# The end of a head pair's attention on VectorE in 18 pieces instead of 10, and a long projection group put first in a pair's second cycle

## The reference

```python
x = x + attn_a(layernorm(x))      # causal attention, 16 heads of 64
x = x + ffn(layernorm(x))         # named f1 in the kernel
x = x + attn_b(layernorm(x))      # a retention scan along the tokens, gated; no scores
x = x + ffn(layernorm(x))         # named f2 in the kernel

# attn_a: q, k, v = x Wq', x Wk', x Wv', split into 16 heads
scores = where(causal, q k' / 8, -inf)
out = (softmax(scores) v) Wo'

# ffn: also attention, not causal, over its 2048 tokens. Each of its four projections
# has a main weight plus two experts of rank 16 chosen from the mean of the tokens:
q = (x Wqm' + gate-weighted (x Vg') Sg Ug' + b) / 8      # k, v likewise
out = o_projection(softmax(q k') v)
```

## Time and profile before

| What | Value |
|---|---|
| profiled execution, span of core 5 | 2594.22 us, 2592.5 us |
| spans of the 8 cores | 2567.9 to 2592.5 us |
| mean granted TensorE clock of the cores | 0.944 to 0.951 |
| PE busy | 2201.5 us, 85% |
| ACT busy | 1498.3 us, 58% |
| DVE busy | 1317.0 us, 51% |
| POOL busy | 635.0 us, 24% |
| DMA | 58 GB/s in the mean |

### The profile page before, as it was taken

The page is one execution under the profiler, slowest core; times in us unless marked ns, Lnnn a source line. Parts: engine busy times, 40 slices in busy tenths (PEclk is TensorE's granted clock), DMA queues, the critical chain, the costliest instruction groups (busy, mean ns, idle before and its releaser), DMA issues.

```text
span 2592.5 us, 39690 instructions; the slowest of 8 cores (2567.9 to 2592.5 us)
## 1 busy us (share of the span) xinstructions
PE 2201.5 (85%) x13480; PEld 766.5 (30%) x13480; DVE 1317.0 (51%) x2018; ACT 1498.3 (58%) x1494; POOL 635.0 (24%) x762
## 2 busy tenths in 40 slices
PE   4888799998699989879899599996989989788886
PEld 2322222223342222222222244443422222222222
DVE  4367635656453444434554567775445454433443
ACT  1234377773007777879999032221057777899991
POOL 4244333434111111112212323333021211021112
PEclk9989899999699999999999899997999999999998
DMA  8111322224400000012211531135200000021003
GB/s 173 25 25 25 62 46 65 66 74 129 148 9 24 25 26 25 17 49 58 58 42 50 130 73 66 65 114 154 74 25 26 25 25 17 17 74 33 33 33 122
DMA packets 49570, 151.10 MB, mean 58 GB/s; under 512 B 6624, under 2 KB 8800, under 8 KB 49120
## 3 DMA queue, kind: packets, MB, share of 16 engines
q1 hardware_dynamic: 33984, 124.80, 14.8%
q0 software_dynamic: 13376, 23.07, 6.1%
q10 hardware_dynamic: 2016, 0.70, 0.1%
HBM read 138.06 MB, written 33.55 MB: 66 GB/s over the span
## 4 chain that ended last, share of the span: by engine, by line
PE 59%; ACT 12%; DVE 12%; issue 8%; DMA 5%; POOL 3%; ACTq 0%; DVEq 0%; POOLq 0%; SPq 0%
ACT MISC L1135 11%; PE psd L1045 10%; PE psx L1064 8%; PE psx L974 6%; PE psx L970 6%; PE psx L1079 6%; PE psx L992 4%; PE psd L965 3%; PE psx L1000 3%; PE psx L965 3%; PE psd L1000 3%; PE psx L978 1%; DVE MISC L1316 1%; DMA XB<-Xs 1%; DVE MISC L1309 1%
## 5 line engine op out<-in xcount | busy, mean ns | idle before, releaser
L1135 ACT ACTIVATE MISC<-psd,NEGC 128x1024 bf16<-128x1024 f32 (+3 forms) x1344 | 1389.0, 1083 | 659.8 <-PE psd L1047 644.0
L1045 PE MATMUL psd<-MISC,KT 64*128 64x512 bf16 (+3 forms) x1344 | 510.2, 382 | 96.5 <-ACT MISC L1135 88.7
L1047 PE MATMUL psd<-MISC,KT 64*128 64x512 bf16 (+3 forms) x1344 | 514.8, 385 | 0.0
L1064 PE MATMUL psx<-MISC,VT 128*64 128x512 bf16 (+3 forms) x1344 | 424.1, 391 | 19.2 <-POOL MISC L1528 7.4
L1066 PE MATMUL psx<-MISC,VT 128*64 128x512 bf16 (+3 forms) x1344 | 425.9, 392 | 0.0
L1045 PEld LDWEIGHTS psd<-MISC,KT 64*128 64x128 bf16 x1344 | 124.4, 93 | 610.7 <-issue 603.5
L1521 POOL TENSOR_TENSOR MISC<-KT 128x512 bf16<-128x512 bf16 x96 | 108.3, 1128 | 565.8 <-DVE KT L1223 507.8
L1316 DVE COPY MISC<-MISC 32x512 f32<-32x512 f32 x384 | 218.6, 569 | 9.1
L1079 PE MATMUL psx<-MISC,ONESs 128*32 128x512 bf16 (+3 forms) x2688 | 218.9, 388 | 0.0
L1521 POOL TENSOR_TENSOR MISC<-MISC 128x512 bf16<-128x512 bf16 x96 | 106.8, 1113 | 339.2 <-DVE MISC L1230 282.4
L1309 DVE RECIPROCAL MISC<-MISC 128x128 f32<-128x128 f32 x192 | 170.0, 922 | 4.6
(11 more groups left out here) (187 smaller groups left out, 2707.6 us busy)
## 6 DMA issues: line engine op xcount, KB each, us to landing
XB<-Xs SPq DMA_DIRECT2D x40, 512.0 KB, 4.1
MISC<-fWq SPq DMA_DIRECT2D x32, 512.0 KB, 3.5
Xs<-XA SPq DMA_DIRECT2D x24, 512.0 KB, 3.0
Xs<-XB SPq DMA_DIRECT2D x24, 512.0 KB, 3.0
XB<-xin SPq DMA_DIRECT2D x16, 512.0 KB, 6.3
XA<-xin SPq DMA_DIRECT2D x16, 512.0 KB, 5.1
MISC<-fWk SPq DMA_DIRECT2D x16, 512.0 KB, 3.6
y<-XB SPq DMA_DIRECT2D x16, 512.0 KB, 3.0
```

What stands on the lines that cost most here:

```text
L1045: mm(pd[:, s:CH], ks[0:64, :], q[0:64, cl * CH + s:(cl + 1) * CH], start=True, stop=True, tile_position=(0, 0))
L1047: mm(pd[:, CH + s:2 * CH], ks[64:128, :], q[64:128, cl * CH + s:(cl + 1) * CH], start=True, stop=True, tile_position=(64, 0)).then_inc(sSC, 1)
L1064: mm(PVB[cl][0:64, s:CH], va[:, 0:64], r[:, s:CH], start=(c.tk == 0), stop=lastk, tile_position=(0, 0))
L1135: s_.activation(r, pd, AF.Exp, bias=NEGC[:, col:col + 1], scale=sc).then_inc(aEX, 1)
```

## The change

Three edits. The first concerns the planner's choice, the other two the pieces at a pair's end.

```diff
@@ fill(k), in attention()
                 e = min(heads, key=queue.index)
+                if cyc[k].tk == 1 and spare >= 1:
+                    e = heads[0]
             it = e[0]
...
@@ close(c), in attention()
-            for i in range(10):
-                P.delay(1 + i * min(c.g.n - 2, 10) // 10, "gn", "gn", c.g, i)
+            for i in range(18):
+                P.delay(2 + i * (c.g.n - 3) // 18, "gn", "gn", c.g, i)
...
@@ VectorE's program, step "gn"
-                    if i < 4:
+                    if i < 8:
                         v.wait_ge(vGE, 3 * g.gi)
-                        d = DN[:, i * 128:(i + 1) * 128]
+                        d = DN[:, i * 64:(i + 1) * 64]
                         chain(v_.reciprocal(d, d))
                         gn_at[i] = nself[0]
-                    elif i < 8:
-                        v.wait_ge(vSF, gn_at[3])
-                        cl = (i - 4) // 2
-                        for q in range(2 * (i % 2), 2 * (i % 2) + 2):
-                            q0 = 64 * cl + 32 * (q // 2)
-                            ins = v_.tensor_copy(RB[cl][32 * q:32 * q + 32, :], DN[q0:q0 + 32, :])
-                        chain(ins)
+                    elif i < 16:
+                        v.wait_ge(vSF, gn_at[7])
+                        cl, q = (i - 8) // 4, i % 4
+                        q0 = 64 * cl + 32 * (q // 2)
+                        chain(v_.tensor_copy(RB[cl][32 * q:32 * q + 32, :], DN[q0:q0 + 32, :]))
                         gn_at[i] = nself[0]
                     else:
-                        cl = i - 8
-                        v.wait_ge(vSF, gn_at[5 + 2 * cl])
+                        cl = i - 16
+                        v.wait_ge(vSF, gn_at[11 + 4 * cl])
```

## The result

The changed kernel's four runs gave 2556.66 to 2561.43 us, median **2557.39**; its profiled execution took 2558.04 us. The runs of the kernel before that can be compared with them, here and beside the first experiments, lie at 2583 to 2592 us, its profiled one aside. The ratio after/before is **0.9896 [0.9872, 0.992]**: 1.0% faster, about 27 us, which is within the 2% that one measurement can tell from no change, though its interval excludes 1.

What follows compares the result with a forecast made beforehand. TensorE, waiting for VectorE at pair ends, bounds a0, a1, f1-0 and f2-0; ScalarE paces f1-1 and f2-1. Terms -19.9 - 15.4 - 10.3 - 2.4 + 2 + 1.7 + 1.8 = -42.5 us take 2594.2 to 2552 us; range 2532 to 2580.

Steps and rivals of the forecast that it cites:

- choice in tk 1: f1-0 and f2-0, 12 pair starts: K before EQ removes waits of 1.66 us each, -19.9 us.
- clock: f1-0 and f2-0: with the waits gone, ten slow TensorE stretches of 1.54 us vanish, -15.4 us.
- a0: Stage a0: seven waits shrink as the first piece comes later, -10.3 us; pieces at other places cost +1.7 us.
- a1: Stage a1: four waits each lose one reciprocal, 3.4 us, less 1 us for late pieces: -2.4 us.
- late pieces in f1-0, f2-0: Pieces in tk 9 to 13 of 16-cycle pairs: 0.2 us in each of 10 pairs with EK, +2 us.
- eight short reciprocals: Eight short reciprocals for four long ones cost 0.3 us more at each of six stage ends, +1.8 us.
- rival A: Waits go but the clock stays low, its falls caused by the whole thin stretch at a pair's end; 2567 us, 20%.
- D: New choice does nothing in tk 1, EQ goes first, waits shrink by only 0.87 us each; 2576 us, 7%.
- The pieces at other places: Forecast step on moved pieces: +2 us in 16-cycle pairs, tight at tk 11, and +1.7 us in a0.
- rival C: Slower: late pieces hold up emptyings in the crowded end of pairs; 2623 us at three quarters exposure, 6%.
- Rival B: a0 gains more: two thirds of its 16 us clock loss return and late pieces are free; 2538 us, 22%.

Runs made afterwards that it cites:

- the first experiments: Only the new choice in tk 1 against the kernel before, 2559.29 us (0.9899); and the changed kernel without that choice, 2563.01 us (0.9916).
- the choice alone: Kernel before with only the new choice in cycle tk 1, ten old pieces left in place: 2559.29 us median, ratio 0.9899; f1-0 and f2-0 283.1 us each.
- the pieces alone: Changed kernel with the old choice, so only the 18 pieces differ from the kernel before: 2563.01 us median, ratio 0.9916.
- the delay alone: Kernel before with only its ten old pieces one cycle later, old choice: 2547.04 and 2566.02 us, no ratio; stage sum 2540.9 us.
- the short squares: Changed kernel with GpSimd's squares on 64 of 512 columns, score bound mostly left out: 2528.86 us, total not comparable; same edit in kernel before: 2568.89 us.
- ten pieces: Kernel before with the new choice and its ten old pieces one cycle later: 2542.44 us median, ratio 0.9833; repeated on another occasion, ratio 0.9806.

## Why the prediction was right or wrong

The forecast, 2552 us, was 5.4 us below the median, inside the range and on the right side of the 2%. That it came so near is in part luck. The change gave about 27 us against the runs of before, and 28.5 us in the stages, where the forecast had 42.5. The profiled execution of before, from which the forecast subtracted, was some 8 us above its neighbours, and that hid half of the error. The error itself is in the terms:

| Term | forecast | measured | how |
|---|---|---|---|
| choice in tk 1 | -19.9 | about -15.2 | 12 x (10.43 - 9.16) |
| clock | -15.4 | -15.4 | clock of f1-0 at 1.00 |
| a0 | -10.3 + 1.7 | -5.3 | stage |
| a1 | -2.4 | -4.0 | stage |
| late pieces in f1-0, f2-0 | +2 | +10.0 | 2 x (288.1 - 283.1), against the choice alone |
| eight short reciprocals | +1.8 | about 0 | below |

The measured terms add up to -29.9 us, 12.6 short of the forecast; 1.4 us of the difference to the stages' 28.5 no row accounts for.

**The choice** did what the diff says, and the two waits went. Its size was too large: of the 1.66 us a pair, 0.27 + 0.28 us came back as waits for ScalarE in tk 3 and 4. (By these rows 1.11 us would be left; measured are 1.27, and the 0.16 us between I can't place.) The forecast had let ScalarE's seven exponentials run from start to end and had found 0.8 us of room over the whole stretch; it had not asked whether the room was there in each cycle. So this term, too, was mis-sized, by 4.7 us.

**The clock** came back whole, so rival A is out; D is out because K's first half stands in tk 1. My argument for the clock was right only in part. The later waits of 1.1 us before line 978 weren't followed by a fall, and the wait of 0.47 us that the later start leaves isn't either, while ten of the twelve long ones on core 5 were (eleven of 1.47 us and one of 1.29 us). The clock records of all eight cores say the same for f1-0 and f2-0. In the kernel before, 74 of the 96 waits of 1.29 or 1.47 us have a fall, which begins between 0.2 us before and 0.9 us behind the wait's end. In each of the two kernels whose wait at this place is 0.28 to 0.47 us (the pieces alone, the delay alone) none of 96 has one. So the runs point to this wait's length, and not to whether there is one, and the choice was not needed for it.

**The failed step is "The pieces at other places".** It put the late pieces at +2 us in f1-0 and f2-0, and they cost 10.0. The forecast had 0.36 us of delay on EK's emptying and 0.2 us a pair on TensorE, with copies at the mean of 0.57 us from the earlier trace rows. That mean mixes two kinds: copies with GpSimd quiet, 0.42 us, and copies beside a GpSimd instruction, here 1.16 us for the second of the two. Which kind one gets depends on what stands beside it. At tk 11 Q's emptying ends, and that one event starts both the copies (next in VectorE's program) and the square on GpSimd (which waits for it). They met in every pair looked at: TensorE's wait behind them is 0.85 us in all five pairs of f1-0 that have EK. From the start of Q's emptying to that of EK's it was 1030.81 - 1029.28 = 1.53 us; the forecast had 1.89, measured are 1010.62 - 1008.20 = 2.42, and TensorE waits 0.85 us a pair instead of 0.2. With the short squares it is 1.69 and no wait. So a pair takes 42.8 us where the forecast named 41.5: 0.85 us here and 0.4 us in the choice. The square could be seen in the trace of before, 0.2 us behind the end of Q's emptying, at 1030.03; at this place I had not looked at GpSimd:

```profile
1030.24 1.04 POOL L1521 TENSOR_TENSOR MISC<-MISC 128x512 bf16<-128x512 bf16 x1 [4.03 <-DVE MISC L1230]
```

The short squares showed the cause, and moving the two pieces away the price (f1-0 at 283.8). The direction was rival C's, its size far smaller: against the versions with ten pieces the late pieces cost 10 us in the f stages, 2 to 3 in a1 and 0 to 2 in a0, 15 at most where C had 61 to 81, because of the places in an f pair that hold late pieces only one was exposed.

**a0 and a1.** The waits in tk 1 and 2 went as forecast (11.35 to 1.15 us, 10.2 of 10.3). But TensorE's idle time in the stage went only from some 35 to 30 us on core 5; the new delays are 5 us where I had put 1.7. VectorE's row at the end of tk 5 there, and TensorE behind it (before: 1.05 us at this place):

```profile
193.78 0.42 DVE L1318 COPY MISC<-MISC 32x512 f32<-32x512 f32 x1
194.23 2.49 DVE L1327 TENSOR_TENSOR XB<-MISC 128x512 bf16<-128x512 f32 x2
196.64 1.27 DVE L1338 BATCH_NORM_STATS2 STT<-XB 128x6 f32<-128x512 f32 x2
198.14 0.67 DVE L1275 COPY XA<-psx 128x1024 bf16<-128x1024 bf16 x1
```

```profile
198.96 1.44 PE L968 MATMUL psx<-W,XA 128*128 128x512 bf16 x3 [3.42 <-DVE XA L1275]
```

Two multiplications that I had priced at 2 x 0.73 take 2.49 us, and behind them, before T's copy, stand two more instructions of 1.27 us. The squares have a part in this too: one of 1.21 us starts on GpSimd at 193.89, and with the short squares the same two multiplications take 1.77 us. In a1 the later start gives 6.3 us (ten pieces: 249.8) and the 18 late pieces take 2.3 back. Rival B, a0 giving more with its clock, did not happen: on core 5 the clock stays at 0.90, and the median of the cores is 0.94 before and 0.92 after.

**Eight short reciprocals.** The forecast's upper bound, a fixed part of 0.16 us each, was too careful by far. At the end of a stage all come in one go; first the changed kernel's, then those of the kernel before:

```profile
602.94 3.43 DVE L1312 RECIPROCAL MISC<-MISC 128x64 f32<-128x64 f32 x8
```

```profile
611.42 3.39 DVE L1309 RECIPROCAL MISC<-MISC 128x128 f32<-128x128 f32 x4
```

Four more instructions, 0.04 us more. A fixed part is there when one stands alone: 0.55 us for 64 columns against 0.95 us for 128. Back to back it does not show. By the Trainium skill (VectorE: DVE Perf Modes, section "The TRN2 errata — SBUF-src ops pay a fixed extra latency per instruction") four more would have cost an estimated 0.24 us; the trace does not agree, and the measurement decides.

**What stays open.** The 5.7 us outside the six stages, the clock of a0, and why 22 of the 96 long waits left the clock alone.

## What to carry to other kernels

Before work is spread out finely, try to move its start by one step: here that alone, with the old ten pieces, took 37.8 us off the four stages, where all three edits took 28.8. When a copy is put behind an emptying, look at what else that emptying releases on GpSimd, and take the copy's price from rows where that neighbour runs, not from the line's mean. And when a wait goes, ask of the next engine whether it has room in each cycle, not over the stretch.

## What the hardware showed that I had not expected

- Two 32 x 512 fp32 copies of VectorE in a row took 0.88 us beside a GpSimd instruction of 0.40 us and 1.61 us beside one of 1.15 us, in the same order of work; a single copy alone took 0.42 us.
- In f1-0 and f2-0 TensorE's clock fell at 74 of 96 waits of 1.29 or 1.47 us on the eight cores, and at none of twice 96 waits of 0.28 to 0.47 us at the same place.
- In one execution two cores of a die stood at a clock of 0.81 for 120 us, while the other two of that die did not.
- Eight reciprocals of 64 columns take as long as four of 128: 3.43 and 3.39 us.
